# Relation shared sums: three of eight one-hots made on ScalarE, block numbers loaded 32 at a time

## Chip, core and metric

The kernel runs on one core of one Trainium2 chip, as one launch. The metric is the device time of that launch in microseconds, the median of some runs. A NeuronCore has five engines with queues of their own: TensorE (PE in the profile, its weight loads as PEld, its sequencer as PEq), VectorE (DVE), ScalarE (ACT), GpSimd (POOL) and SyncE (SP), which here only issues transfers.

## What is computed

Four graph networks are applied one after another to 3125 nodes of 64 features and 103125 edges sorted by destination. The change lies in the last one, two layers of relational attention. Its core, cut from the reference:

```
attn = ex / (denom[dst] + 1e-16)
out_j = xw[etype, src].reshape(-1, H, hc // H)          # H = 4 heads, hc = 64
agg = segment_sum(attn[:, :, None] * out_j, dst, num_segments=n)
return agg.reshape(n, hc) + b
```

So for each edge a row of 64 numbers, chosen by relation type and source, is weighted by one share per head, and the rows are summed into the node to which the edge points.

## The kernel before

Edges are cut into 832 chunks of 128, so that no chunk crosses a block of 125 destination nodes. Eight chunks make a group (`HALF = 8`), of which there are 104. A sum over destinations is done by TensorE: a one-hot matrix `S` (128 edges x 125 places in the block, fp32) is the weight, the messages `M` (128 x 68: 64 features and 4 shares) are the moving data, and the result is added in PSUM at the columns of the chunk's block.
The stage of the change is `shared_sums` (from line 1833 on). It is used four times: twice for the pair attention, with `with_self=True` (from 6140 and 8259 us in the trace; here called the sister stage), and twice for the relations, with `with_self=False` (from 10159 and 11736 us). The relation form works so, for each of 26 rounds (`LT`) of four groups (`HT`), each with a slot of its own in `G`, `S` and `M`:

- SP loads the kept rows of a group (`load_rows`, line 1863), as soon as the messages of the group four before are made.
- VectorE waits until TensorE has done the group four before (`chunk_done`, line 1904), makes all eight one-hots in one comparison (`make_onehots`, line 560, instruction at 562: 128 x 1000), waits for the rows, copies the shares (line 1921) and makes the messages (line 1922).
- TensorE (from line 1949 on) reads 16 block numbers ahead of every second group (line 1955, instruction at 527), waits for the one-hots and messages of the group (lines 1959 to 1961), and issues eight chunks (`sum_chunk`, line 576).
- ScalarE and GpSimd have no program in this form. In the sister form the one-hots come from DRAM, and ScalarE makes part of the products, with a copy of the shares first (lines 1934 to 1940).

Ahead of the loop TensorE zeroes seven PSUM banks (`zero_sums`, line 572), and behind it VectorE copies all sums out (line 1926). Every stage is a block of its own, with all engines meeting at its end. Each engine runs its program in order. The order across engines is set by semaphores alone; there is no planner.

Of the kernel before, what the change touches and what calls it, by code (L numbers as in the profile page):

```python
# [13 lines left out]
F32 = mybir.dt.float32  # L14
BF16 = mybir.dt.bfloat16
I32 = mybir.dt.int32
ACT = mybir.ActivationFunctionType
AX = mybir.AxisListType.X

P = 128  # L20
# [3 lines left out]
BN = 125  # L24
# [6 lines left out]
HALF = 8  # L31
K = 4
U = K * HALF
TURNS = NCH // U
GROUPS = NCH // HALF
PAIR = 2 * HALF
# [19 lines left out]
def build(nc, io, out):  # L56
    ctx = ExitStack()
    with ctx:
        phase = [0]

        def sb(name, shape, dt=F32, stack=ctx, side=None):
            return stack.enter_context(nc.sbuf_tensor(f"{name}_{phase[0]}", shape, dt, side=side))
# [26 lines left out]
        pos = sb("pos", [P, P])  # L89
        part = sb("part", [P, 1])  # L90
        dloc = sb("dloc", [P, NS])
# [25 lines left out]
        def link(ins):  # L117

            steps[0] += 1
            ins.then_inc(dve_step, 1)  # L120
            nc.vector.wait_ge(dve_step, steps[0])
# [387 lines left out]
        onehot_made = Counted("onehots_made")  # L509
        chunk_done = Counted("chunks_done", U)  # L510
# [14 lines left out]
        def blocks_of(chunk, n, row=None, most=NB - 1):  # L525

            return nc.values_load_multi_w_load_instructions(
                (rows[0:1, 0, :] if row is None else row)[:, bass.ds(chunk, n)], engines=[mybir.EngineType.PE], min_val=0, max_val=most,
                skip_runtime_bounds_check_because="blocks are counted below NB")[1]

        def group_of(k):
            return slice(HALF * k, HALF * (k + 1))
# [24 lines left out]
                                                bass.IndirectOffsetOnAxis(IDX[:, k, q:q + 1], 0)  # L557
                                                ).then_inc(gathered[k].sem, 16)

        def make_onehots(S, i, k, pos):  # L560

            return nc.vector.tensor_tensor(
                S[:, group_of(k), :], pos[:, 0:BN].unsqueeze(1).to_broadcast([P, HALF, BN]),
                dloc[:, bass.ds(i * U + HALF * k, HALF)].unsqueeze(2).to_broadcast([P, HALF, BN]), ALU.is_equal)

        def load_onehots(sp, S, i, k):
            sp.dma_start(S[:, group_of(k), :].rearrange("p c d -> p (c d)"),
# [6 lines left out]
        def sum_chunk(ps_sum, S, j, M, width, at):  # L574

            return nc.tensor.matmul(ps_sum[0:BN, bass.ds(at, width)], S[:, j, :], M,  # L576
                                    start=False, stop=True, skip_group_check=True)

        def sums(ps_sum, width):
            return ps_sum[0:BN, 0:NB * P].rearrange("p (b f) -> p b f", f=P)[:, :, 0:width]  # L580
# [852 lines left out]
        last_added = Counted("last_heads_added")  # L1433
        folded = Counted("heads_folded")
        own_copied = Counted("own_shares_copied")
        shares_kept = Counted("shares_kept")
        reduced = Counted("scores_reduced")
        rows_turned = Counted("fetched_rows_turned", 1)
# [399 lines left out]
        def shared_sums(SUM, SCORE, heads, width, stash, with_self, last_load=None):  # L1838
# [4 lines left out]
            out_w = D + heads  # L1843
            HT = 4
            LT = GROUPS // HT
            arrived = loaded
            es = ExitStack()
            with es:
# [4 lines left out]
                DH = heads - 2  # L1853
                SH = sb("shares_half", [P, 2, HALF, heads - DH], F32, es) if with_self else None
                AO = 2 * HALF
                zero = sb("zero_bank", [P, BANK], F32, es)
                ps_sum = pb("ps_sum", [P, 7 * BANK], F32, es)
                ready, finished = (once(x) for x in ("set_up", "loop_over"))
                with nc.Block() as block:
# [31 lines left out]
                    @block.vector  # L1891
                    def _(dve):
                        v = nc.vector
                        v.memset(zero[:, :], 0.0).then_inc(ready, 1)
                        with dve.Fori(0, LT) as i:
                            for h in range(HT):
                                n = HT * i + h + 1
                                half = slice(HALF * h, HALF * (h + 1))
                                share = SCORE[:, bass.ds(HALF * (HT * i + h), HALF), :]

                                dve.wait_ge(chunk_done.sem, chunk_done.at(HALF * (HT * (i - 1) + h + 1)))
                                if not with_self:
                                    make_onehots(S, i, h, pos).then_inc(onehot_made.sem, 1)
                                dve.wait_ge(arrived[h].sem, arrived[h].at(16 * i + 16))
                                if with_self:

                                    dve.wait_ge(msg_made.sem, msg_made.at(n - 2))
                                    v.tensor_tensor(PR[:, h % 2, :, 0:DH, :], G[:, half, 0:DH * D].rearrange("p c (h f) -> p c h f", f=D),
                                                    share[:, :, 0:DH].unsqueeze(3).to_broadcast([P, HALF, DH, D]), ALU.mult).then_inc(mult_made.sem, 1)
                                    v.tensor_scalar(M[:, half, D:out_w], share[:, :, heads:2 * heads], 1.0, None, ALU.mult).then_inc(own_copied.sem, 1)  # L1910

                                    dve.wait_ge(act_multiplied.sem, act_multiplied.at(AO * n))
                                    dve.wait_ge(mult_made.sem, mult_made.at(n))
                                    v.tensor_tensor(PR[:, h % 2, :, 3, :], PR[:, h % 2, :, 3, :], PR[:, h % 2, :, 4, :], ALU.add).then_inc(last_added.sem, 1)
                                    dve.wait_ge(mult_made.sem, mult_made.at(n))
                                    dve.wait_ge(last_added.sem, last_added.at(n))
                                    v.tensor_tensor(PR[:, h % 2, :, 0:2, :], PR[:, h % 2, :, 0:2, :], PR[:, h % 2, :, 2:4, :], ALU.add).then_inc(folded.sem, 1)
                                    dve.wait_ge(folded.sem, folded.at(n))
                                    v.tensor_tensor(M[:, half, 0:D], PR[:, h % 2, :, 0, :], PR[:, h % 2, :, 1, :], ALU.add).then_inc(msg_made.sem, 1)
                                else:  # L1920
                                    v.tensor_scalar(M[:, half, D:out_w], share, 1.0, None, ALU.mult).then_inc(own_copied.sem, 1)
                                    v.tensor_tensor(M[:, half, 0:D].rearrange("p c (h f) -> p c h f", h=heads),
                                                    G[:, half, 0:D].rearrange("p c (h f) -> p c h f", h=heads),
                                                    share.unsqueeze(3).to_broadcast([P, HALF, heads, D // heads]), ALU.mult).then_inc(msg_made.sem, 1)
                        dve.wait_ge(finished, 1)
                        link(v.tensor_copy(SUM[:, :, :], sums(ps_sum, out_w)))

                    if with_self:
                        @block.scalar
# [13 lines left out]
                    @block.tensor  # L1943
                    def _(pe):
                        for c in (msg_made, chunk_done):
                            nc.tensor.nop().then_inc(c.sem, c.credit)
                        pe.wait_ge(ready, 1)
                        zero_sums(ps_sum, zero, 7)
                        with pe.Fori(0, LT) as i:
                            for h in range(HT):  # L1950
                                for q in range(HALF):
                                    j = HALF * h + q
                                    if q == 0 and h % 2 == 0:
                                        at = blocks_of(HALF * (HT * i + h), PAIR)
                                    if q == 0:
                                        if with_self:
                                            pe.wait_ge(onehots_in[h].sem, onehots_in[h].at(16 * i + 16))
                                        else:
                                            pe.wait_ge(onehot_made.sem, onehot_made.at(HT * i + h + 1))
                                        pe.wait_ge(msg_made.sem, msg_made.at(HT * i + h + 1))  # L1960
                                        pe.wait_ge(own_copied.sem, own_copied.at(HT * i + h + 1))
                                    sum_chunk(ps_sum, S, j, M[:, j, :], out_w, at[j % PAIR] * P).then_inc(chunk_done.sem, 1)
                        nc.tensor.matmul(ps_sum[:, 6 * BANK + 3 * P:7 * BANK], zero[:, 0:P], zero[:, 0:P], start=False, stop=True,
                                         skip_group_check=True).then_inc(finished, 1)
                for c in arrived:
# [3 lines left out]
                if with_self:  # L1969
                    for c in (mult_made, last_added, folded, shares_kept):  # L1970
                        c.over(GROUPS)
                    act_multiplied.over(AO * GROUPS)
                    for c in onehots_in:
                        c.over(16 * LT)
                else:
                    onehot_made.over(GROUPS)

        until_stored = ExitStack()
        masks_stored = segments_phase()
# [242 lines left out]
```

## Time and profile before

| | us |
|---|---|
| median of 3 runs | 9910.92 (9910.38 to 9911.04) |
| profiled execution, span | 11974.2 |
| relation shared sums, first | 10159 to 10379 |
| relation shared sums, second | 11736 to 11956 |
| pair-attention shared sums (sister), two | from 6140 and from 8259 |

The profiled execution is one run of the same program with the hardware profiler on, which is longer than the timed ones. In the rows below "busy" is the time in which an engine had an instruction in hand. PEclk is TensorE's granted clock as a share of 2.4 GHz: 1.00 is 2.4 GHz, 0.50 is 1.2 GHz. "idle before" is the time in which the engine had nothing, and behind the arrow stands what the profile takes to have ended it. "issue" means that nothing the profile shows was waited for, which includes the engine's own sequencer still being at work.

### The profile page before, as it was taken

How to read it: one execution, taken by the hardware profiler on the slowest of the kernel's cores; microseconds unless marked ns; L12 is line 12 of the kernel's file. 1: busy time of each engine (PE TensorE's matmuls, PEld its weight loads, DVE VectorE, ACT ScalarE, POOL GpSimd, SP SyncE). 2: the span in 40 equal slices, each digit the busy share in tenths (PEclk: the TensorE clock that was granted, in tenths of full speed). 3: DMA queues.
4: the chain of work that ended last, by engine and by line, in shares of the span. 5: the costliest groups of instructions: out<-in, count | busy, mean ns of one | idle time of the engine just before them, and what ended most of it. 6: DMA issues, size and time to landing. Idle time of an engine off the chain costs nothing. (4 is left out here: it accounts for less than half of the span.)

```text
span 11974.2 us, 162471 instructions
## 1 busy us (share of the span) xinstructions
PE 7534.2 (63%) x38295; PEld 5244.5 (44%) x38296; DVE 7367.7 (62%) x10447; ACT 2310.3 (19%) x8712; POOL 5383.2 (45%) x5649
## 2 busy tenths in 40 slices
PE   2878788667677775555548555554855554855557
PEld 1666566555555552333347323333732222622226
DVE  6665433355555555677799567778955555745558
ACT  0222344300000001111159111114910000000000
POOL 2555555455545543665400266550015553055550
PEclk9888888788878885777755577775557666867768
DMA  2333344344444444766649566664933333333333
GB/s 60 87 84 84 99 114 114 90 113 111 110 95 113 111 96 163 234 233 231 194 203 411 179 232 232 229 216 173 415 120 74 74 73 63 116 72 75 75 72 100
DMA packets 851293, 1717.47 MB, mean 143 GB/s; under 512 B 384638, under 2 KB 473541, under 8 KB 796922
## 3 DMA queue, kind: packets, MB, share of 16 engines
q1 hardware_dynamic: 465500, 1137.96, 27.5%
q0 software_dynamic: 207456, 413.40, 15.8%
q10 hardware_dynamic: 178256, 165.14, 4.1%
q8 instruction: 37, 0.61, 0.0%
q14 instruction: 44, 0.35, 0.0%
HBM read 1263.59 MB, written 453.99 MB: 143 GB/s over the span
## 5 line engine op out<-in xcount | busy, mean ns | idle before, releaser
L556 POOL DMA_INDIRECT gathered_rows<-node_table,index x2496 | 2379.1, 953 | 2000.0 <-issue 652.4
L719 PE MATMUL ps_G<-table_parts,low_onehots 125*128 125x320 bf16 x15600 | 2712.0, 336 | 294.1 <-issue 220.8
L576 PE MATMUL ps_sum<-messages,onehots 128*125 128x65 f32 (+3 forms) x13312 | 2113.4, 321 | 993.1 <-issue 643.6
L576 PEld LDWEIGHTS ps_sum<-messages,onehots 128*125 128x125 f32 x13312 | 2011.7, 236 | 1117.9 <-issue 1111.2
L556 POOL DMA_INDIRECT gathered_rows<-xl_table,index x1664 | 1576.7, 948 | 1828.5 <-issue 1028.0
L556 POOL DMA_INDIRECT gathered_rows<-rel_table,index x1456 | 1391.9, 956 | 2009.8 <-ACT index L546 1020.9
L1524 PE MATMUL ps_Z<-xr,onehots_wide 125*128 x3328 | 1505.3, 610 | 1194.5 <-issue 628.4
L719 PEld LDWEIGHTS ps_G<-table_parts,low_onehots 125*128 125x128 bf16 x15600 | 1677.7, 110 | 1183.2 <-issue 312.8
L749 DVE TENSOR_TENSOR rows_by_feature<-ps_G,fifth_onehots 128x320 f32<-128x320 f32 x1040 | 507.0, 487 | 2271.9 <-remote 1683.0
L1524 PEld LDWEIGHTS ps_Z<-xr,onehots_wide 125*128 125x128 f32 x3328 | 801.4, 257 | 1899.3 <-issue 1802.7
L1572 DVE TENSOR_TENSOR z<-gathered_rows,ps_Z 128x650 f32<-128x650 f32 x832 | 670.9, 828 | 835.4 <-issue 499.7
L1693 PE MATMUL ps_W<-w,fetched_turned 64*128 64x512 f32 x416 | 420.2, 1098 | 660.1 <-issue 539.8
L1940 ACT ACTIVATE products<-kept_rows,shares_half 128x64 f32<-128x64 f32 x3328 | 817.3, 334 | 34.3 <-DMA kept_rows<-stash_a 25.1
L1584 DVE TENSOR_REDUCE scores_quad<-z 128x20 f32<-128x1280 f32 x416 | 615.4, 1479 | 0.0
L1579 DVE SCALAR_TENSOR_TENSOR z<-z,ps_att 128x1280 f32<-128x1280 f32 x416 | 614.5, 1477 | 0.0
L1544 ACT ACTIVATE score<-ps_Z 128x10 f32 (+1 forms) x832 | 149.8, 180 | 2226.2 <-remote 816.1
L729 DVE TENSOR_TENSOR low_onehots<-low_rows,ps_ids 125x1280 bf16<-125x1280 f32 (+1 forms) x416 | 476.7, 1146 | 103.1 <-DMA low_rows<-low_rows 58.7
L546 ACT ACTIVATE index<-src_all 128x8 int32 (+1 forms) x640 | 126.8, 200 | 2057.5 <-issue 1977.5
L1736 ACT ACTIVATE fetched_turned<-ps_X 64x128 f32<-64x128 f32 x208 | 56.4, 271 | 2196.5 <-remote 1056.6
L836 ACT ACTIVATE messages<-gathered_rows,weights 128x64 f32<-128x64 f32 x1664 | 419.7, 335 | 28.8 <-ACT weights L831 8.5
L752 DVE TENSOR_REDUCE gathered_rows<-rows_by_feature 128x64 f32<-128x320 f32 x832 | 404.5, 486 | 28.5
L1776 DVE TENSOR_TENSOR rows_by_type<-ps_W,onehots_type 128x544 f32<-128x544 f32 x208 | 150.8, 725 | 416.3 <-remote 340.1
(326 smaller groups left out, 7209.2 us busy)
## 6 DMA issues: line engine op xcount, KB each, us to landing
stash_a<-gathered_rows SPq DMA_DIRECT2D x208, 1300.0 KB
kept_rows<-stash_a SPq DMA_DIRECT2D x208, 1300.0 KB
onehots<-onehots_kept SPq DMA_DIRECT2D x520, 500.0 KB
onehots_turned<-onehots_turned SPq DMA_DIRECT2D x416, 250.0 KB
stash_r<-gathered_rows ACTq DMA_DIRECT2D x208, 272.0 KB
kept_rows<-stash_r SPq DMA_DIRECT2D x208, 272.0 KB
low_rows<-low_rows SPq DMA_DIRECT2D x416, 125.0 KB
onehots_kept<-onehots ACTq DMA_DIRECT2D x104, 500.0 KB
```

The lines of the kernel that those rows point to most:

```text
L556: pool.indirect_dma_start(G[:, HALF * k + q, 0:width], None, table, bass.IndirectOffsetOnAxis(IDX[:, k, q:q + 1], 0)).then_inc(gathered[k] ...
L576: return nc.tensor.matmul(ps_sum[0:BN, bass.ds(at, width)], S[:, j, :], M, start=False, stop=True, skip_group_check=True)
L719: last = nc.tensor.matmul(ps_G[:, (fetch * k + g) % 2, 0:D * FIVE], OT[0:BN, k, g, a, :], HP[:, part, a, :, :].rearrange("p f b -> p (f b) ...
L729: v.tensor_tensor(OT[0:BN, k, :, :, :], LR[0:BN, k, :].rearrange("p (g e) -> p g e", e=P).unsqueeze(2).to_broadcast([BN, fetch, FIVE, P]), ...
L749: v.tensor_tensor(BR[:, (fetch * k + g) % 2, :, :], ps_G[:, (fetch * k + g) % 2, 0:D * FIVE].rearrange("p (f b) -> p f b", b=FIVE), HI[:, ...
L836: last = nc.scalar.activation(M[:, HALF * k + q, 0:D], G[:, HALF * k + q, :], ACT.Copy, scale=W[:, k, q:q + 1])
L1524: last = nc.tensor.matmul(ps_Z[:, m % 2, q, 0:PW], SW[0:BN, j % WIDE, :], XR[:, bass.ds(at[j % PAIR] * PW, PW)], start=True, stop=True)
L1572: v.tensor_tensor(Z[:, p % ZB, 2 * e:2 * e + 2, :], G[:, j:j + 2, :], ps_Z[:, e, :, 0:GW], ALU.add).then_inc(z_made.sem, 1)
L1579: v.scalar_tensor_tensor(z, z, 0.0, ps_att[:, 0:FA].unsqueeze(1).to_broadcast([P, QD, FA]), ALU.max, ALU.mult).then_inc(mult_made.sem, 1)
L1584: v.tensor_reduce(RED[:, p % 2, :, :], Z[:, p % ZB, :, 0:FA].rearrange("p c (h f) -> p c h f", f=D), AX, ALU.add).then_inc(reduced.sem, 1)
L1693: nc.tensor.matmul(ps_W[:, 0:D * R], XT[:, k % 2, :], by_type, start=True, stop=True)
L1940: nc.scalar.activation(PR[:, h % 2, q, k, :], G[:, HALF * h + q, k * D:(k + 1) * D], ACT.Copy, scale=SH[:, h % 2, q, k - DH:k - DH + 1]).t ...
```

## The change

In the relation form VectorE makes only the first five of a group's eight one-hots (`HALF - OWN`, with `OWN = 3`). ScalarE gets a program: per group it waits for the free slot, copies the eight columns of places (`dloc`) to a tile, waits for itself, makes three tiles of distances |place - position| with Abs (bias from the tile, scale -1), waits for itself, and turns the three together into one-hots with Relu(1 - distance). TensorE waits for both engines' one-hots. It reads 32 block numbers ahead of every fourth group (`PL = HT`) instead of 16 ahead of every second. The sister form keeps its code.

```diff
-        def make_onehots(S, i, k, pos):
+        def make_onehots(S, i, k, pos, count=HALF):
             return nc.vector.tensor_tensor(
-                S[:, group_of(k), :], pos[:, 0:BN].unsqueeze(1).to_broadcast([P, HALF, BN]),
-                dloc[:, bass.ds(i * U + HALF * k, HALF)].unsqueeze(2).to_broadcast([P, HALF, BN]), ALU.is_equal)
+                S[:, HALF * k:HALF * k + count, :], pos[:, 0:BN].unsqueeze(1).to_broadcast([P, count, BN]),
+                dloc[:, bass.ds(i * U + HALF * k, count)].unsqueeze(2).to_broadcast([P, count, BN]), ALU.is_equal)
...
+                PL = 2 if with_self else HT
+                OWN = 0 if with_self else 3
+                DL = None if with_self else sb("places", [P, HT, HALF], F32, es)
+                AW = None if with_self else sb("distances", [P, HT, OWN, BN], F32, es)
...
-                                    make_onehots(S, i, h, pos).then_inc(onehot_made.sem, 1)
+                                    make_onehots(S, i, h, pos, HALF - OWN).then_inc(onehot_made.sem, 1)
...
+                    if not with_self:
+                        @block.scalar
+                        def _(act):
+                            with act.Fori(0, LT) as i:
+                                for h in range(HT):
+                                    n = HT * i + h + 1
+                                    act.wait_ge(chunk_done.sem, chunk_done.at(HALF * (HT * (i - 1) + h + 1)))
+                                    nc.scalar.activation(DL[:, h, :], dloc[:, bass.ds(HALF * (HT * i + h), HALF)], ACT.Copy).then_inc(shares_kept.sem, 1)
+                                    act.wait_ge(shares_kept.sem, shares_kept.at(n))
+                                    for q in range(OWN):
+                                        last = nc.scalar.activation(AW[:, h, q, :], pos[:, 0:BN], ACT.Abs, scale=-1.0,
+                                                                    bias=DL[:, h, HALF - OWN + q:HALF - OWN + q + 1])
+                                    last.then_inc(distance_made.sem, 1)
+                                    act.wait_ge(distance_made.sem, distance_made.at(n))
+                                    nc.scalar.activation(S[:, HALF * (h + 1) - OWN:HALF * (h + 1), :], AW[:, h, :, :], ACT.Relu, scale=-1.0, bias=1.0
+                                                         ).then_inc(act_onehot_made.sem, 1)
...
-                                    if q == 0 and h % 2 == 0:
-                                        at = blocks_of(HALF * (HT * i + h), PAIR)
+                                    if q == 0 and h % PL == 0:
+                                        at = blocks_of(HALF * (HT * i + h), HALF * PL)
...
                                             pe.wait_ge(onehot_made.sem, onehot_made.at(HT * i + h + 1))
+                                            pe.wait_ge(act_onehot_made.sem, act_onehot_made.at(HT * i + h + 1))
...
-                                    sum_chunk(ps_sum, S, j, M[:, j, :], out_w, at[j % PAIR] * P).then_inc(chunk_done.sem, 1)
+                                    sum_chunk(ps_sum, S, j, M[:, j, :], out_w, at[j % (HALF * PL)] * P).then_inc(chunk_done.sem, 1)
```

## Rows read from the trace of the kernel before

**Rows 1.** The page: span, then busy time, share and instructions of each engine.

```profile
span 11974.2 us, 162471 instructions
...
PE 7534.2 (63%) x38295; PEld 5244.5 (44%) x38296; DVE 7367.7 (62%) x10447; ACT 2310.3 (19%) x8712; POOL 5383.2 (45%) x5649
```

**Rows 2.** Stretches, relation stages: length, busy PE, PEld, DVE, ACT, POOL, PEclk, DMA.

```profile
10168.00:10376.00 208.00, 190.85 (x1654) 184.04 (x1654) 186.41 (x306) 0.00 (x0) 0.00 (x0) 1.00 0.48 133
11744.00:11952.00 208.00, 190.86 (x1652) 183.81 (x1651) 185.08 (x303) 0.00 (x0) 0.00 (x0) 1.00 0.48 131
```

**Rows 3.** Order of time, first relation stage: start, length, engine, line, operation.

```profile
10167.76 7.10 PE L576 MATMUL ps_sum<-messages,onehots 128*125 128x68 f32 x64
...
10251.97 3.70 PE L576 MATMUL ps_sum<-messages,onehots 128*125 128x68 f32 x32 [0.18 <-issue]
...
10254.07 1.20 DVE L562 TENSOR_TENSOR onehots<-pos,dloc 128x1000 f32<-128x1000 f32 x1 [0.20 <-PE ps_sum L576]
...
10255.87 1.19 DVE L562 TENSOR_TENSOR onehots<-pos,dloc 128x1000 f32<-128x1000 f32 x1
...
10256.18 3.70 PE L576 MATMUL ps_sum<-messages,onehots 128*125 128x68 f32 x32 [0.51 <-DVE messages L1922]
...
10260.04 3.70 PE L576 MATMUL ps_sum<-messages,onehots 128*125 128x68 f32 x32 [0.15 <-issue]
```

**Rows 4.** Groups of instructions, 10168 to 10378: busy us, mean ns, idle before.

```profile
L576 PE MATMUL ps_sum<-messages,onehots 128*125 128x68 f32 x1663 | 192.2, 274 | 17.1 <-DVE messages L1922 12.8 <-issue 2.9 <-DVE messages L1921 0.2
...
L562 DVE TENSOR_TENSOR onehots<-pos,dloc 128x1000 f32<-128x1000 f32 x102 | 122.1, 1197 | 16.8 <-PE ps_sum L576 16.8
L1922 DVE TENSOR_TENSOR messages<-kept_rows,score 128x512 f32<-128x512 f32 x102 | 69.9, 685 | 0.0
```

**Rows 5.** Single lines, sequencer work: duration ns min/median/max, first and last start.

```profile
L527 PEldq TENSOR_LOAD <-rows x1: 1107/1107/1107, 10254.6 to 10254.6; - x1
...
L527 PEldq TENSOR_LOAD <-rows x51: 1102/1106/1117, 10169.4 to 10371.9; - x51
...
L972 ACTq TENSOR_LOAD <-rows x208: 304/309/532, 2337.2 to 4434.1; - x104
...
L1949 PEldq ALU_OP  x1: 32/32/32, 10254.1 to 10254.1; - x1
L1949 PEldq COMPARE_BRANCH  x1: 207/207/207, 10254.2 to 10254.2; - x1
```

**Rows 6.** Order of time of ScalarE, first sister stage.

```profile
6251.77 0.22 ACT L1935 ACTIVATE shares_half<-score 128x16 f32 x1 [0.27 <-DVE messages L1919]
6252.11 3.93 ACT L1940 ACTIVATE products<-kept_rows,shares_half 128x64 f32<-128x64 f32 x16
```

**Rows 7.** Groups of instructions of ScalarE, whole span.

```profile
L1539 ACT ACTIVATE onehots_wide<-onehots_turned 125x256 f32<-125x256 bf16 x832 | 339.5, 409 | 11.2 <-DMA onehots_turned<-onehots_turned 8.5 <-issue 2.7
...
L824 ACT ACTIVATE onehots_narrow<-onehots 128x1000 bf16<-128x1000 f32 x104 | 106.1, 1020 | 4.3 <-DMA onehots<-onehots_kept 4.3
...
L428 ACT ACT_TABLE_LOAD x3 | 3.8, 1283 | 30.8 <-PEq L1169 22.4 <-PEq L193 5.1 <-PEq L604 3.2
```

**Rows 8.** Stretches: start and middle of the first sister stage, and a dense stage.

```profile
6152.00:6154.00 2.00, 0.89 (x4) 0.90 (x5) 1.97 (x3) 2.00 (x10) 0.00 (x0) 0.69 1.01 420
...
6200.00:6550.00 350.00, 282.55 (x1249) 267.71 (x1249) 338.03 (x391) 324.00 (x1328) 0.00 (x0) 0.50 1.01 412
...
10400.00:10450.00 50.00, 50.00 (x94) 24.08 (x94) 23.30 (x77) 5.13 (x19) 0.00 (x0) 0.50 0.27 102
```

**Rows 9.** Order of time of PE, first sister stage.

```profile
6153.11 3.62 PE L576 MATMUL ps_sum<-messages,onehots 128*125 128x69 f32 x16 [3.90 <-DVE messages L1919]
6157.56 3.62 PE L576 MATMUL ps_sum<-messages,onehots 128*125 128x69 f32 x16 [0.83 <-DVE messages L1919]
...
6180.04 2.37 PE L576 MATMUL ps_sum<-messages,onehots 128*125 128x69 f32 x10 [0.82 <-DVE messages L1919]
```

**Rows 10.** A stretch of the second weighted-sums stage.

```profile
1988.00:1989.00 1.00, 0.28 (x4) 0.30 (x4) 0.69 (x2) 0.00 (x0) 0.77 (x1) 0.75 0.41 131
```

**Rows 11.** Order of time of PE in the first and second weighted-sums stage.

```profile
419.10 1.95 PE L576 MATMUL ps_sum<-messages,onehots 128*125 128x65 f32 x16 [1.09 <-issue]
...
1986.05 1.96 PE L576 MATMUL ps_sum<-messages,onehots 128*125 128x65 f32 x16 [1.46 <-issue]
```

More of the change, by code:

```diff
@@ L1435, in build @@
         own_copied = Counted("own_shares_copied")
+        act_onehot_made = Counted("onehots_of_scalar")
+        distance_made = Counted("distances_made")
         shares_kept = Counted("shares_kept")
@@ L1975, in shared_sums @@
                 else:
-                    onehot_made.over(GROUPS)
+                    for c in (onehot_made, act_onehot_made, distance_made, shares_kept):
+                        c.over(GROUPS)
         until_stored = ExitStack()
```

## Prediction, before the change was run

> **What bounds the kernel now.** I began with the page [rows 1]: the profiled span is 11974.2 us, the median of the runs shown 9910.92, so the profiler adds 2063 us over the whole program. It doesn't say where. I make the sum on the profiled span and add the difference in microseconds, unscaled, to 9910.92, because what it charges is time of the array itself. The change touches only the two relation shared-sum stages, 10160 to 10378 and 11737 to 11954.
>
> The stretches table [rows 2] shows that PE is busy for 190.85 of 208 us in either, at a granted clock of 1.00, so at 2.4 GHz. DVE is busy for 186, ScalarE for nothing. Both PE and DVE look nearly full, so the order of time has to decide [rows 3]. PE takes a pair of groups in 3.70 us (32 matmul records, two for a chunk), then idles 0.15 or 0.51 in turn: pairs start at 10251.97, 10256.18 and 10260.04, which is 8.07 us for four groups. DVE needs 1.80 us for a group (one-hots 10254.07 to the next at 10255.87), 7.20 for four, and then waits for PE. The table of groups [rows 4] charges 12.8 us of PE's idle time to the DVE messages. I read that otherwise: the one-hots of 10254.07 start when the first group of PE's pair ends, and fill its slot, so they are four groups ahead; what PE needs at 10256.18 was made before them. What holds PE is its own sequencer. It reads 16 block numbers for a pair, 1.10 us [rows 5]: from 10254.6 to 10255.7, behind the loop's end at 10254.1 and a branch of 0.21, then 0.5 us of register work and waits. That chain lasts 10256.18 - 10254.1 = 2.08 us, of which the matmuls still queued (done at 10255.67) hide 1.57. In the other pair no branch stands ahead, and 0.15 shows. PE and its number load set the pace, DVE isn't the bound.
>
> **DVE's one-hots, 8 to 5.** 1000 elements take 1197 ns, 512 of messages 685 [rows 4]: 1.05 ns each, so 625 take 0.80 us, 0.39 less, and four groups of DVE fall from 7.20 to 5.6 us. On the path that is worth nothing: it lengthens the wait for PE. The wait that moves is only DVE's idle.
>
> **ScalarE.** Idle here; now a Copy, three Abs and a Relu per group. The sister stage (shared sums of the attention layers) has [rows 6] 0.34 us from the share copy to the first product, and 16 products of 64 columns in 3.93 us, so 0.24 from one to the next. An Abs of 125 columns is some 0.05 wider: three take 0.95. The Relu of 375 lies between 409 ns (256 columns) and 1020 (1000) [rows 7]: 0.51. With a wait between, about 1.9 us for a group, 7.6 for four; bounds 1.6 and 2.2 for the unseen functions and waits. It starts when a slot is freed and is needed three groups (over 5 us) later, so it is hidden. Behind its waits nothing is queued. Copy, the only function the loops use, needs no table load in any of them; the loads stand at the norms and softmaxes, 1283 ns each [rows 7]; that Abs and Relu need none no row shows. The Trainium skill, "ScalarE: Activation LUTs", section on table sets, lists cheap functions (relu, copy, abs) in every set, by which the loop has none.
>
> **TensorE's extra wait.** One ALU step of 32 ns and a semaphore per group, issued ahead while matmuls are queued: nothing, or 0.05 us at the head of four. SP's loads wait for messages as before, which come no later.
>
> **The number load is the step that counts.** 104 loads of 16 become 52 of 32. A load of 4 numbers takes 304 ns on ScalarE's sequencer, one of 16 takes 1102 on PE's [rows 5]: 66.5 ns for each number and 38 fixed. So 32 take 2.17 us, 1.06 more. No row has 32: bounds are 1.10 (the count doesn't matter) and 2.21 (two of 16); I take 2.17, since the two sizes lie on a line through almost zero. So the reading isn't saved, it is put in one place, where one queue's worth of matmuls covers it, not two. The Trainium skill, "Runtime: NRT & Kernel Launch", section "Instruction fetch mechanics", gives about 200 ns per register; by it the 16 more numbers would cost 3.2 us instead of 1.06, but 1102 ns for 16 contradicts it and I don't use it.
>
> At full clock four groups then run as one stream of 3.70 x 2 - 0.30 = 7.10 us (as the first 64 records do, at 10167.76 [rows 3]), then idle 0.51 + 1.06 = 1.57: 8.67 instead of 8.07. That alone is 0.60 x 52 = +31 us.
>
> **What the longer gap does to the clock.** This is the larger term. In the sister stage the same fp32 chunk matmuls, 16 records in 3.62 us, are followed by gaps of 0.83 [rows 9]. There the clock falls after an idle of 3.90, is 0.69 in the mean of 6152 to 6154, and is 0.50 from 6200 to 6550 throughout, with PE busy for 282 of the 350 us [rows 8]. In the second weighted-sums stage 16 such records in 1.96 us come after an idle of 1.46 [rows 11], and the clock falls behind them, 0.75 from 1988 to 1989 [rows 10]; the same at 1681 and 1834 (three in all). So chunk matmuls lose the full clock around a gap of 1.46; 0.51, the longest in the steady relation stage, lets them keep it. A gap of 1.57 is the one of [rows 11] again. Full clock would be lost within the first groups. Would it come back? The zeroing matmuls (512 columns) brought it at the start; chunk matmuls at 0.50 never did in the sister stage, and a dense stage with PE busy for 50.00 of 50 us stays at 0.50 [rows 8]. I take it that it doesn't.
>
> At 1.2 GHz 16 records take 3.62, and 10 take 2.37 [rows 9]: some 0.21 apart, twice the 0.106 of full clock (7.10 less 3.70, over 32; so 0.2125 below). Four groups: 3.62 + 48 x 0.2125 = 13.8 us. The sequencer's chain is now 2.08 + 1.06 = 3.14 us, but the dozen queued records cover 12 x 0.2125 + 0.42 = 2.97 of it; a gap of 0.17 is left. Four groups: 13.97. With two of a stage's 26 rounds still at full clock: 24 x 13.97 + 2 x 8.67 = 352.6, against 26 x 8.07 = 209.8: +142.8 a stage, +286 for both. 11974 becomes 12260, and 9911 becomes **10197**. What follows each stage runs at 0.50 already (H and dense) or is DVE work, so nothing more moves. If all is slow from the start it is +307; if the unprofiled stage before runs at DVE's 7.20, its floor, 45 more; if the clock takes ten rounds to fall, 80 less. Own range 10110 to 10250.
>
> **Rivals.**
> A. The clock holds: the gap of 1.57 comes once in 8.67 us, and a gap of 1.09 [rows 11] passed without a fall in the first weighted-sums stage (among bf16 matmuls of 320 columns). Then +31 us, 9942. The Trainium skill, "TensorE: Matmul & The Clock Gate", section "HAM oscillation", would have only idle gaps longer than this one bring the clock down, which is this rival. The first idle of [rows 11] and the fall of [rows 10] speak against it.
> B. The clock comes and goes, about half the time low: +31 + 130, some 10070. A stream of 14 us without a gap at 0.50 is something no row of chunk work shows.
> C. The load doesn't grow with the count: the gap is 0.51 once in four groups, 7.61 instead of 8.07, -0.46 x 52 = -24 us: 9887. DVE at 5.6 and ScalarE at 7.6 would just follow. It decides for C when a load of 32 takes under 1.7 us (8.07 - 7.10 = 0.97 = 0.51 + 0.46).
> D. ScalarE becomes the bound, through table loads inside the loop: two more of 1.28 us make a group 4.5 us, against 2.02 now: +2.5 x 208 = +520. From 2.02 us a group it costs at full clock, from 3.5 at half.
> E. What the change is said to do, relieving DVE and halving the loads, does nothing: DVE wasn't late, and the gaps of one long load and of two short ones come out alike. Then 0, 9911.
>
> **How the numbers follow.** Forecast 0.67, A 0.13, B 0.07, C 0.08, D 0.03, E or else 0.02. Range 9930 to 10250: it takes in the forecast, A and B, and leaves out C, D and the edges. 0.2% (20 us) is about what can be told from no change. Faster is C's larger part, 0.06; same is the rest of C, E, and a little of A, 0.05; slower 0.89.
>
> **What would show it.** PEclk near 0.5 in both stages, L576 with 68 columns at a mean of about 420 ns instead of 274, four groups in 14 us, a stage in some 350; 26 number loads a stage of about 2170 ns; one-hots of DVE 0.80 us, with long waits for PE; ScalarE busy some 45% or less of the stage. PEclk at 1.00 with gaps of 1.57 is A, loads of about 1100 ns are C, table loads in the loop D. I am most exposed in the clock: if gaps without the profiler are well below 1.57, A is what is timed, even where the trace shows the fall.

## The result, and the profile after

The changed kernel takes 10178.29 us (median of 4 runs, 10176.85 to 10179.23), the kernel before 9910.98: ratio 1.0269, 95% interval 1.0255 to 1.0284, so +267 us. The forecast was 10197, slower by 286.

The page after: its span, and the busy time of each engine with its share and instructions.

```profile
span 10176.2 us, 164553 instructions
...
PE 7595.6 (75%) x38295; PEld 5411.8 (53%) x38296; DVE 7288.7 (72%) x10447; ACT 2662.8 (26%) x9752; POOL 5380.1 (53%) x5649
```

The groups of instructions of the first relation stage, 8372 to 8725, with busy us, mean ns of one, and idle time before; they answer to [rows 4]:

```profile
L576 PE MATMUL ps_sum<-messages,onehots 128*125 128x68 f32 x1664 | 342.4, 410 | 1.1 <-DVE messages L1927 1.1
...
L1945 ACT ACTIVATE distances<-pos,places 128x125 f32<-128x125 f32 x312 | 101.9, 390 | 3.4
L562 DVE TENSOR_TENSOR onehots<-pos,dloc 128x625 f32<-128x625 f32 x104 | 84.3, 811 | 182.3 <-PE ps_sum L576 182.3
...
L1949 ACT ACTIVATE onehots<-distances 128x375 f32<-128x375 f32 x104 | 53.7, 516 | 3.3
```

One matmul record of a chunk has gone from 274 ns to 410, TensorE has no idle time left but one gap of 1.1 us, and DVE waits for it for 182 us of a stage in which it waited for 17. The order of time shows where that begins, in the first and in the second stage (start, length, and in brackets the idle time before):

```profile
8380.75 7.10 PE L576 MATMUL ps_sum<-messages,onehots 128*125 128x68 f32 x64
8388.96 91.26 PE L576 MATMUL ps_sum<-messages,onehots 128*125 128x68 f32 x438 [1.11 <-DVE messages L1927]
...
9813.17 7.10 PE L576 MATMUL ps_sum<-messages,onehots 128*125 128x68 f32 x64
9821.32 78.99 PE L576 MATMUL ps_sum<-messages,onehots 128*125 128x68 f32 x385 [1.06 <-DVE messages L1927]
```

64 records at full clock, one gap of 1.1, and from there a stream with no gap and a record each 0.21 us (334 us by 1593 records). The stretches around it (length, busy PE, PEld, DVE, ACT, POOL, then PEclk) answer to [rows 2]:

```profile
8386.00:8390.00 4.00, 2.89 (x27) 2.76 (x26) 2.99 (x6) 3.61 (x11) 0.00 (x0) 1.00 0.57 166
8390.00:8392.00 2.00, 2.00 (x12) 2.00 (x12) 0.26 (x1) 0.23 (x2) 0.00 (x0) 0.51 0.56 163
...
8390.00:8724.00 334.00, 334.00 (x1593) 334.00 (x1593) 143.67 (x288) 163.58 (x480) 0.00 (x0) 0.50 0.28 78
```

The clock is 1.00 up to 8390 and 0.50 (1.2 GHz) for the 334 us that follow, with PE busy for every one of them. The closing matmul of the first stage stands in the two traces, after and before, as

```profile
8724.03 0.73 PE L1988 MATMUL ps_sum<-zero_bank 128*128 128x128 f32 x2
...
10377.04 0.44 PE L1963 MATMUL ps_sum<-zero_bank 128*128 128x128 f32 x2
```

So the first stage, from its first chunk to its closing matmul, takes 8724.03 - 8380.75 = 343.3 us, where before it took 10377.04 - 10167.76 = 209.3. The second takes 342.1, where before it took 209.3. Together that is +266.8 us, the whole result.

The single lines of the number load (duration min/median/max) and of the loop's end ahead of that first gap, for [rows 5]:

```profile
L527 PEldq TENSOR_LOAD <-rows x26: 2129/2132/2145, 8373.2 to 8707.3; - x26
...
L527 PEldq TENSOR_LOAD <-rows x1: 2137/2137/2137, 8386.2 to 8386.2; - x1
...
L1973 PEldq ALU_OP  x1: 32/32/32, 8385.7 to 8385.7; - x1
```

One reading was spoilt from the start. The span of the profile before, 11974.2 us, is not the profiler's doing: the profiled run after spans 10176.2 us and is as long as the timed ones. In some executions the program takes some 11900 us whatever the kernel (so in experiment 12, for both kernels), with idle times of 2.4 us between gathers, while the relation rounds take what they take otherwise.

### The profile page after: what moved, and what is told of

It is laid out like the page before. It is cut to its first block and busy times, and to the rows that moved or that the text cites. A ratio compares the mean times of both kernels' runs of the same rounds, so it can differ in the third digit from the quotient of the medians.

```text
span 10176.2 us, 164553 instructions
## 1 busy us (share of the span) xinstructions
PE 7595.6 (75%) x38295; PEld 5411.8 (53%) x38296; DVE 7288.7 (72%) x10447; ACT 2662.8 (26%) x9752; POOL 5380.1 (53%) x5649
## 5 line engine op out<-in xcount | busy, mean ns | idle before, releaser
L576 PE MATMUL ps_sum<-messages,onehots 128*125 128x65 f32 (+3 forms) x13312 | 2280.3, 348 | 461.0 <-DVE messages L1925 182.1
L576 PEld LDWEIGHTS ps_sum<-messages,onehots 128*125 128x125 f32 x13312 | 2196.5, 262 | 580.9 <-issue 574.7
L1526 PE MATMUL ps_Z<-xr,onehots_wide 125*128 x3328 | 1393.3, 577 | 769.2 <-DVE z L1574 683.5
L1526 PEld LDWEIGHTS ps_Z<-xr,onehots_wide 125*128 125x128 f32 x3328 | 769.6, 243 | 1393.4 <-issue 1270.0
L546 ACT ACTIVATE index<-kept_types 128x8 int32 (+1 forms) x216 | 44.4, 208 | 1686.6 <-DMA gathered_rows<-rel_table,index 1647.2
L562 DVE TENSOR_TENSOR onehots<-pos,dloc 128x625 f32<-128x625 f32 x208 | 168.6, 811 | 364.0 <-PE ps_sum L576 364.0
L1025 DVE TENSOR_TENSOR messages<-gathered_rows,ps_A 128x512 f32<-128x512 f32 x208 | 143.0, 688 | 397.3 <-DMA gathered_rows<-node_table,index 391.4
```

The costliest lines, as they stand in the source:

```text
L1526: last = nc.tensor.matmul(ps_Z[:, m % 2, q, 0:PW], SW[0:BN, j % WIDE, :], XR[:, bass.ds(at[j % PAIR] * PW, PW)], start=True, stop=True)
```

## Experiments

All take the kernel before or the changed one and edit the relation form of `shared_sums` alone. Times are medians; differences are against the kernel before, run on the same chip in between. "Round" is four groups.

**1. ScalarE's one-hots alone.**

```diff
# changed kernel
-                PL = 2 if with_self else HT
+                PL = 2
```

> Only ScalarE's one-hots: three of eight made there, block numbers still read 16 ahead of every second group. Theory (the long number load makes a gap, and the gap takes the clock down): the gaps stay at 0.15 and 0.5 us, PEclk stays 1.00 in both relation stages, time within 10 us of the kernel before, since DVE was not late. Rival (ScalarE's one-hots are the cause, by a later release of TensorE or by the wait for a second engine): all or most of the +267 us is here, with PE waiting for ScalarE.

Measured: 10150.9 against 9901.6, +249 us (ratio 1.0256, 1.0239 to 1.0273). Mine was wrong, the rival's number right. Order of time of PE:

```profile
8375.83 3.70 PE L576 MATMUL ps_sum<-messages,onehots 128*125 128x68 f32 x32 [0.64 <-ACT onehots L1949]
8379.92 3.70 PE L576 MATMUL ps_sum<-messages,onehots 128*125 128x68 f32 x32 [0.38 <-ACT onehots L1949]
8384.36 3.70 PE L576 MATMUL ps_sum<-messages,onehots 128*125 128x68 f32 x32 [0.74 <-ACT onehots L1949]
8388.46 3.70 PE L576 MATMUL ps_sum<-messages,onehots 128*125 128x68 f32 x32 [0.40 <-ACT onehots L1949]
8392.95 107.26 PE L576 MATMUL ps_sum<-messages,onehots 128*125 128x68 f32 x518 [0.78 <-ACT onehots L1949]
```

The gaps of 0.15 and 0.51 [rows 3] have become 0.4 and 0.75, a round takes 8384.36 to 8392.95 = 8.59 us instead of 8.07, and after some rounds the clock falls. ScalarE, which the brackets name, isn't late:

```profile
8386.46 0.21 ACT L1942 ACTIVATE places<-dloc 128x8 f32 x1 [0.94 <-PE ps_sum L576]
...
8387.71 0.52 ACT L1949 ACTIVATE onehots<-distances 128x375 f32<-128x375 f32 x1
```

It had waited for PE to free the slot by the first group of the pair of 8384.36. What it then makes, ready at 8388.23, is for the group four after that one, two groups later than the one that PE begins at 8388.46. The change of 0.52 us a round goes with four waits more, 0.13 us each.

**2. The number load alone.**

```diff
# kernel before
-                                    if q == 0 and h % 2 == 0:
-                                        at = blocks_of(HALF * (HT * i + h), PAIR)
+                                    if q == 0 and h % HT == 0:
+                                        at = blocks_of(HALF * (HT * i + h), HALF * HT)
```

> Only the number load: 32 ahead of every fourth group, all eight one-hots on DVE. Theory: PEclk falls to 0.50 at the first gap of about 1.1 us, each stage takes 343 us, +267 us over the kernel before, the same as the whole change. Rival (ScalarE is the cause): within 35 us of the kernel before, which would be what the gap itself costs at full clock.

Measured: 10165.1, +264 us (1.0268, 1.0251 to 1.0285), as my theory had it. Its first gap is 0.97:

```profile
8368.76 7.10 PE L576 MATMUL ps_sum<-messages,onehots 128*125 128x68 f32 x64
8376.83 123.57 PE L576 MATMUL ps_sum<-messages,onehots 128*125 128x68 f32 x594 [0.97 <-DVE messages L1924]
```

Either half of the change by itself loses nearly all of the 267 us: they don't add up, since the clock falls only once. What the long load alone would cost at full clock isn't shown, since the one round at full clock is the stage's first. It takes 8.07 us, where the first round of the kernel before takes 10175.14 - 10167.76 = 7.38 and only its later ones 8.07:

```profile
10175.14 3.70 PE L576 MATMUL ps_sum<-messages,onehots 128*125 128x68 f32 x32 [0.28 <-issue]
```

**3. Eight numbers ahead of every group.** As 2, with `h % 1` and `HALF`.

> The other direction: 8 numbers ahead of every group, all one-hots on DVE. A load of 8 should take 0.57 us (2132 ns for 32, 1102 for 16, 304 for 4) and hide wholly under queued matmuls. Theory: no gaps, PEclk 1.00, TensorE could do four groups in 6.94 us, so DVE with 7.20 us sets the pace: 0.87 us less for each of 52 rounds, -45 us. Rival (the number of loads costs, not their length): 208 loads are slower than 104, +10 us or more.

Measured: 10130.9, +229 us (1.0229, 1.0212 to 1.0246): the rival's direction, and beyond. The load of 8 takes 591 ns, but does not hide.

```profile
8386.76 8.10 PE L576 MATMUL ps_sum<-messages,onehots 128*125 128x68 f32 x64 [0.51 <-DVE messages L1924]
8395.38 104.85 PE L576 MATMUL ps_sum<-messages,onehots 128*125 128x68 f32 x507 [0.51 <-DVE messages L1924]
```

64 records take 8.10 us here instead of 7.10, by small holes at every group's head, and a round takes 8.62. Two loads more cost 0.55 us, 0.27 each beside their numbers. So TensorE's sequencer is not hidden behind matmuls: what is added to it lengthens the round. Gaps of 0.51 kept the clock in the kernel before; here, with holes between them and the same work in 8.62 us, they don't.

**4. ScalarE's one-hots, and eight numbers per group.** The changed kernel with `PL = 2 if with_self else 1`.

> The changed kernel with 8 numbers ahead of every group: ScalarE makes three of eight one-hots. Theory: PEclk 1.00 again. TensorE at 6.94 us for four groups is nearly the bound, ScalarE's own 1.77 us for a group gives 7.1: -50 us against the kernel before, some 5 to 14 us less than with DVE alone. Rival (ScalarE's part alone takes the clock down or makes TensorE late): slower than the same loads with DVE alone.

Measured: 10163.9, +262 us (1.0266, 1.0249 to 1.0283). Wrong in the same way. It falls sooner than 3, and after shorter gaps than any other run (first stage, then the stretches around its fall, then a round of the second stage):

```profile
8382.03 1.96 PE L576 MATMUL ps_sum<-messages,onehots 128*125 128x68 f32 x16 [0.33 <-ACT onehots L1949]
8384.20 116.10 PE L576 MATMUL ps_sum<-messages,onehots 128*125 128x68 f32 x555 [0.21 <-issue]
...
8384.00:8385.00 1.00, 0.80 (x7) 0.81 (x8) 0.87 (x3) 0.84 (x4) 0.00 (x0) 1.00 0.43 63
8385.00:8386.00 1.00, 1.00 (x7) 1.00 (x7) 0.63 (x2) 0.86 (x3) 0.00 (x0) 0.50 0.61 220
...
9810.14 1.96 PE L576 MATMUL ps_sum<-messages,onehots 128*125 128x68 f32 x16 [0.38 <-ACT onehots L1949]
...
9819.27 1.96 PE L576 MATMUL ps_sum<-messages,onehots 128*125 128x68 f32 x16 [0.63 <-issue]
```

The clock is 1.00 up to 8385 and 0.50 from there, and up to that point the stage has had gaps of 0.33 and 0.21 only. The kernel before keeps the clock with longer ones. So it isn't the longest gap alone that decides; idle time in several small pieces does it too. A round of the second stage takes 9819.27 - 9810.14 = 9.13 us, and the additions of 1 and 3 to 8.07 make 8.07 + 0.52 + 0.55 = 9.14.

**5. One wait for three.** If waits are what costs, fewer must gain:

```diff
# kernel before; DVE's three instructions of a group all count on group_made, SyncE waits for it too
-                                            pe.wait_ge(onehot_made.sem, onehot_made.at(HT * i + h + 1))
-                                        pe.wait_ge(msg_made.sem, msg_made.at(HT * i + h + 1))
-                                        pe.wait_ge(own_copied.sem, own_copied.at(HT * i + h + 1))
+                                            pe.wait_ge(group_made.sem, group_made.at(3 * (HT * i + h + 1)))
```

> The kernel before, with TensorE's three waits per group turned into one: DVE's three instructions of a relation group count on one semaphore, TensorE and SyncE wait for its third count. Number load and one-hots as before. Theory (TensorE's sequencer sets the round: 8.07 us for four groups with 12 waits and two loads, 8.6 with 16 waits in e1, so 0.13 us for each wait): eight waits less leave 7.0 us of sequencer work, so DVE's 7.20 us sets the pace, PEclk 1.00 throughout, 0.87 x 52 = -45 us. Rival (the semaphores cost nothing in the sequencer, e1 was slowed by ScalarE being late): within 10 us of the kernel before.

Measured: 9859.5 against 9897.2, -38 us (0.9964, 0.995 to 0.9978).

```profile
8383.68 14.54 PE L576 MATMUL ps_sum<-messages,onehots 128*125 128x68 f32 x128 [0.18 <-issue]
8398.37 7.20 PE L576 MATMUL ps_sum<-messages,onehots 128*125 128x68 f32 x64 [0.15 <-DVE messages L1922]
```

Two rounds in 14.69, 7.35 each: (8.07 - 7.35) x 52 = 37 us. This is faster than both kernels, though not by the 45 expected: eight waits fewer give 0.72 us, 0.09 each and not 0.13.

**6. One wait, and 32 numbers.** 5 and 2 together.

> e5 with 32 numbers ahead of every fourth group. Sequencer work for four groups about 6.8 us, less than TensorE's 6.94, but a load of 2.13 us in one place, with at most 2.15 us of matmuls queued ahead and 0.6 us of loop end and wait beside it. Theory (the gap in one place decides the clock, not the sum): a gap of 0.4 to 0.7 us, near the edge; if the clock falls, +267 us, if it holds, about -40. Rival (only the sum of sequencer work counts): PEclk 1.00 and -45 us for certain.

Measured: 10163.3, +266 us (1.0271, 1.0254 to 1.0289).

```profile
8381.74 7.20 PE L576 MATMUL ps_sum<-messages,onehots 128*125 128x68 f32 x64 [0.78 <-DVE messages L1924]
8389.71 35.67 PE L576 MATMUL ps_sum<-messages,onehots 128*125 128x68 f32 x175 [0.77 <-DVE messages L1924]
```

Rounds of 7.97 us, shorter than before's 8.07, and the clock still falls at the second gap of 0.77. So the round's length, or the sum of sequencer work in it, doesn't decide alone: idle time gathered in one place does harm, too. That rules out the rival. It also bounds the reading of 3. Against 5 this kernel has one load fewer in a round and the same 32 numbers, and its round is 0.62 us longer, not 0.27 shorter. How long a round is depends on where in it the sequencer's work lies, and not only on what it adds up to.

**7. ScalarE's one-hots with two waits.** The changed kernel with one wait for DVE's three instructions, one for ScalarE, and 16 numbers per pair.

> The changed kernel's ScalarE one-hots, with 16 numbers ahead of every second group and two waits per group (one for DVE's three instructions, one for ScalarE). Theory: sequencer work 8.07 - 4 x 0.13 = 7.55 us for four groups, gaps shorter than in the kernel before, PEclk 1.00, -0.52 x 52 = -27 us: ScalarE's one-hots do no harm by themselves, and gain nothing over e5. Rival (ScalarE's one-hots take the clock down, in whatever way): PEclk 0.50 and +230 us or more.

Measured: 9885.9 against 9897.2, -11 us (0.9989, 0.998 to 0.9999).

```profile
8414.12 7.49 PE L576 MATMUL ps_sum<-messages,onehots 128*125 128x68 f32 x64 [0.41 <-ACT onehots L1950]
8422.02 7.47 PE L576 MATMUL ps_sum<-messages,onehots 128*125 128x68 f32 x64 [0.41 <-ACT onehots L1950]
...
8474.00:8554.00 80.00, 75.27 (x654) 72.55 (x652) 60.52 (x123) 68.48 (x204) 0.00 (x0) 1.00 0.53 142
```

7.9 us a round and the clock at 1.00, where I had expected 7.55 us and -27. ScalarE makes the same three one-hots as in the changed kernel, so their making doesn't take the clock down. Against 5 it costs 26 us: a wait for ScalarE more per group, 0.55 us a round, so 0.14 each. Against 1 two waits for DVE fewer per group give 8.59 - 7.90 = 0.69 us, 0.09 each, as in 5.

**8. The gap filled.** If idleness takes the clock down, useless work in its place must keep it up:

```diff
# changed kernel; ps_fill is the eighth PSUM bank
                                     sum_chunk(ps_sum, S, j, M[:, j, :], out_w, at[j % (HALF * PL)] * P).then_inc(chunk_done.sem, 1)
+                                    if not with_self and h == HT - 1 and q == HALF - 1:
+                                        nc.tensor.matmul(ps_fill[:, :], zero[:, 0:P], zero[:, :], start=True, stop=True)
```

> The changed kernel with one matmul more behind every fourth group (zeros by zeros, 512 columns, fp32, into the eighth PSUM bank, which nobody reads), 0.85 us of TensorE's time at full clock, just where the number load leaves it idle. Theory (the idle gap takes the clock down): the gap is mostly filled, PEclk stays near 1.00, within 30 us of the kernel before though more is computed. Rival (the clock falls for another reason): PEclk 0.50, and 1.7 us more for each of 52 rounds than the changed kernel, +350 us.

Measured: 9919.4 against 9897.2, +22 us (1.0023, 1.0013 to 1.0033).

```profile
8387.30 7.20 PE L576 MATMUL ps_sum<-messages,onehots 128*125 128x68 f32 x64 [0.35 <-DVE messages L1928]
8394.34 1.07 PE L1990 MATMUL ps_fill<-zero_bank 128*128 128x512 f32 x2
8395.76 7.20 PE L576 MATMUL ps_sum<-messages,onehots 128*125 128x68 f32 x64 [0.35 <-DVE messages L1928]
...
8462.00:8542.00 80.00, 76.25 (x618) 68.02 (x618) 55.62 (x112) 62.82 (x186) 0.00 (x0) 1.00 0.49 133
```

The changed kernel with a matmul more is 245 us faster relative to the kernel before. A round takes 8.46 us (some take 8.51), and (8.46 - 8.07) x 52 = 20. This is what the change and the filler together cost with the clock up. The run doesn't tell whether it is the shorter gap or the 1.07 us of wide matmul that keeps it.

**9. The load four numbers longer.** The kernel before, `blocks_of(..., PAIR + 4)` in the relation form, with the last four unused.

> The kernel before, reading 20 block numbers ahead of every second group where 16 are used: only the length of the load changes, by 0.27 us, twice in four groups. Theory (longer idle gaps of TensorE take the clock down, whatever lengthens them; the edge lies between 0.51, which holds in the kernel before, and 0.77, which fell in e6): gaps of 0.42 and 0.78, a fall within some rounds, PEclk 0.50, +230 to +265 us. Rival (only the change's own parts do it, or the edge lies higher): PEclk 1.00, 8.6 us for four groups, +28 us.

Measured: 10172.1 against 9905.4, +267 us (1.0269, 1.0252 to 1.0286). The load takes 1364 ns, the first gap is 0.77:

```profile
8370.41 7.13 PE L576 MATMUL ps_sum<-messages,onehots 128*125 128x68 f32 x64
8378.31 73.06 PE L576 MATMUL ps_sum<-messages,onehots 128*125 128x68 f32 x356 [0.77 <-DVE messages L1924]
```

No wait, no engine and no number of loads is changed here. A quarter of a microsecond more in each load costs as much as the whole change. The gap behind the stage's first round was 0.28 in the kernel before.

**10. Three long rounds, then as before.**

```diff
# kernel before; rounds(i, pl) is the loop's body with pl groups for a load
-                        with pe.Fori(0, LT) as i:
+                        with pe.Fori(0, 3) as i:
+                            rounds(i, HT)
+                        with pe.Fori(3, LT) as i:
+                            rounds(i, 2)
```

> The kernel before, but the first three of a relation stage's 26 rounds read 32 numbers at once, and the other 23 read 16 ahead of every second group, as before. Theory (the clock falls at the first long gap and chunk matmuls at 1.2 GHz don't bring it back): all the stage at PEclk 0.50, four groups in 13.35 us, +265 us, though 23 rounds are the code of the kernel before. Rival (the clock follows the work of the moment): back to 1.00 some rounds after the third, +20 to +40 us.

Measured: 10174.3, +269 us (1.027, 1.0253 to 1.0288). A stretch in the part whose code is that of the kernel before:

```profile
8427.00:8547.00 120.00, 120.00 (x573) 120.00 (x573) 67.83 (x108) 0.00 (x0) 0.00 (x0) 0.50 0.30 83
```

**11. The same, and seven wide matmuls behind the three rounds.**

```diff
+                            for b in range(7):
+                                nc.tensor.matmul(ps_fill[:, :], zero[:, 0:P], zero[:, :], start=True, stop=True)
```

> e10, and behind the three rounds seven matmuls of zeros by zeros (512 columns, fp32, into the eighth PSUM bank, which nobody reads), as many as the zeroing ahead of the loop, before the 23 rounds as before. Theory (wide matmuls without a gap bring the clock back, and the short gaps then keep it): PEclk 1.00 from there on; the cost is 2 x (3 x 5.3 us of slow rounds + 6 us of filler) = +40 us. Rival (something else holds the clock down once it fell): PEclk 0.50 to the end, +275 us.

Measured: 9941.1 against 9905.4, +36 us (1.0035, 1.0021 to 1.0049), where I had +40.

```profile
8384.28 26.18 PE L576 MATMUL ps_sum<-messages,onehots 128*125 128x68 f32 x128 [0.96 <-DVE messages L1922]
8410.26 7.42 PE L1970 MATMUL ps_fill<-zero_bank 128*128 128x512 f32 x14
8417.51 7.10 PE L576 MATMUL ps_sum<-messages,onehots 128*125 128x68 f32 x64
...
8428.00:8548.00 120.00, 109.57 (x948) 105.48 (x947) 109.51 (x180) 0.00 (x0) 0.00 (x0) 1.00 0.50 137
```

128 records in 26.18 us, 7.4 us of wide matmuls, then 64 in 7.10: the clock is back and stays. 10 and 11 run the same code for 23 of 26 rounds and lie 233 us apart.

**12. ScalarE's part without a wait of TensorE.** As 5, with two of eight one-hots on ScalarE; DVE waits for them before its messages.

> e5's single wait and 16 numbers ahead of every second group, with two of eight one-hots on ScalarE; DVE, not TensorE, waits for ScalarE (ahead of its last instruction of the group), so TensorE's sequencer has one wait per group still. Theory (in e5 DVE's 7.2 us and the sequencer's 7.0 lie close together, at 7.35 in all): DVE at 6.2 us and ScalarE at 5.6 drop out, TensorE runs at 7.0 to 7.2 us for four groups with PEclk 1.00: -46 to -56 us against the kernel before, where e5 has -38. Rival (the sequencer alone makes the 7.35): -38 us as e5.

Measured: 11895.8 against 11940.7, -45 us (0.9961, 0.9946 to 0.9976, so -29 to -64). That doesn't tell it from 5, but the trace does:

```profile
10136.94 14.54 PE L576 MATMUL ps_sum<-messages,onehots 128*125 128x68 f32 x128 [0.18 <-issue]
10151.65 7.20 PE L576 MATMUL ps_sum<-messages,onehots 128*125 128x68 f32 x64 [0.16 <-issue]
```

14.71 for two rounds, that of 5. So with one wait, too, DVE isn't what sets the 7.35; relieving it gains nothing. The trace of 5 agrees: DVE makes a group each 1.80 us without a gap up to 8406, and from then on one group in four takes some 1.95, so that there it waits a little for its slot. The rival holds as far as DVE goes. That the sequencer makes the 7.35 is what remains, and isn't shown by itself. ScalarE works here without a wait of TensorE for it, and the round stays that of 5; so the 0.13 us of 1 belong to the wait and not to ScalarE's work.

## Why the prediction was right, point by point

- **PE and its number load set the pace, DVE doesn't.** Right, and in a stronger form. I saw a load that was partly hidden by queued matmuls; 1, 3, 4, 5 and 7 show that work added to the sequencer lengthens the round and work taken off shortens it: 0.13 us for a wait for ScalarE, 0.09 for each of two waits for DVE, 0.27 for a load beside its numbers. It is no plain sum: with the loads put together the round of 6 is longer than that of 5. That the 12.8 us which the profile charged to DVE's messages were the sequencer's work too is my reading; DVE's part stands two groups ahead, and no run singles it out.
- **DVE's one-hots at 0.80 us, nothing on the path.** 811 ns, and 182 us of idle time ahead of them.
- **ScalarE 1.9 us a group, hidden.** In order of time one group has its copy at 8600.05 and its Relu's end at 8601.82: 1.77 us, of a group every 3.36. At full clock, in 7, it still waits for PE (10.6 us in 100). No table load in the loop.
- **The extra wait, "nothing, or 0.05 us".** Mis-sized: 0.13 us each, 0.52 a round, and by 1 that alone brings the clock down. I had taken it as issued ahead, which needs a sequencer with time to spare. Had the load been left as it was, the prediction would have said no change, and would have been wrong by 249 us.
- **The load of 32 numbers, 2.17 us.** 2.13. Loads of 8, 16, 20 and 32 numbers take 591, 1107, 1364 and 2132 ns, 64 ns a number. The line through 4 and 16 held, on another engine.
- **The gap, 1.57 us.** 1.11. The chain from the loop's end is 8388.96 - 8385.7 = 3.3 us, near my 3.14, but 2.15 of it were covered instead of 1.57. That the queue is fuller after a longer stream is my reading; 6 has the same gap after its first and its second round. The +0.60 a round at full clock has no run of its own: 8 shows 0.39 with its filler. Here I was lucky. My rows had the clock held behind a gap of 1.09 and lost behind 1.46, and the gap came out at 1.11, between them; that far less is enough was shown only later, by 4, 6 and 9.
- **The clock falls and doesn't come back.** Right. 9 shows the fall from a longer load alone, 8 that work in the gap prevents it, 10 that chunk matmuls don't bring it back, 11 that wide ones do. It fell at the first gap of either stage, where I had given it two rounds. "Three in all" was a miscount: in the trace before, the clock falls some fifty times between 1240 and 2290.
- **A round at 1.2 GHz, 13.97 us.** 13.44 (ScalarE's copies of four groups apart, 8600.05 and 8613.49): no gap is left, and 0.210 from record to record instead of 0.2125. 25 x 13.44 + 8.2 = 344, measured 343.3. The errors of size go opposite ways: 0.53 us too much for each of 48 slow rounds is 25 us, and a round more at full clock in each stage took some 9 off. That leaves 286 for 267.
- **Rival A**, the full clock holding, is out: gaps of 0.77 us were enough here, in 6 and 9. The Trainium skill's rule in "TensorE: Matmul & The Clock Gate" (section "HAM oscillation"), by which only longer idle gaps bring the clock down, spoke for it; these traces don't agree with it. B (coming and going), C (a load that doesn't grow) and D (table loads) are out by the 334 us at 0.50, by 2132 ns and by the group of ScalarE. The border of C, "under 1.7 us", was a slip: 1.10 and the 0.46 by which the gap could grow make 1.56.
- **"The profiler adds 2063 us"** was wrong, and harmless since the stages were costed in microseconds of their own.

What stays open: why chunk matmuls, which leave no idle time in the records at 1.2 GHz, don't raise the clock where 512 columns do. And what exactly the clock follows. Neither the longest gap nor the round's length orders the runs. The clock holds with gaps of 0.51 and 0.15 in 8.07 us and up to 0.57 at times (the kernel before), with 0.55 in 8.10 (11) and with 0.41 in 7.90 (7). It falls with 0.77 in 7.97 (6), with 0.51 and small holes in 8.62 (3), and after 0.33 and 0.21 with small holes (4).

## What to carry to other kernels

A stage whose matmuls are small (here 68 columns) can hang on the full clock by a few tenths of a microsecond: before lengthening a TensorE gap, by a wait, a register load or a branch, look whether the stage is at 1.00 and whether a neighbour with the same matmuls and longer gaps is at 0.50. Gathering sequencer work in one place lost the clock (2, 6), and so did more pieces of it (3, 4), so count loads and waits first: one semaphore for three instructions of one engine gained 38 us (5). Where a gap can't be shortened, a dummy wide matmul in it is cheap beside the fall: +22 us against the kernel before, where the changed kernel has +267 (8).

## What the runs showed of the hardware that I had not expected

- Both clocks are stable states of the same code: 23 rounds at 1.00 or at 0.50 by what three rounds before them did (10 and 11), 8.1 or 13.4 us each.
- A semaphore wait against a register's value lengthened TensorE's round by 0.13 us (for ScalarE, 1) or 0.09 (for DVE, 5 and 7), and a register load by 0.27 us beside its 64 ns a number (3).
- One idle gap of 0.77 us in each round of 7.97 was enough for the clock to fall (6), where 0.51 in 8.07 was not (the kernel before); in 4 it fell after gaps of 0.33 and 0.21.
